# A second queue for the weight loads of the opening: SyncE keeps the transposes, GpSimd issues the loads, with a new order of loads, buffers and sums

## The reference

```python
def _bitlinear(x, w):
    scale = jnp.mean(jnp.abs(w))
    q = jnp.round(jnp.clip(w / (scale + EPS), -1.0, 1.0))
    deq = q * scale
    return x @ deq.T
gate = _bitlinear(hidden_states, w_gate)
up = _bitlinear(hidden_states, w_up)
inter = gate * up
out = _bitlinear(inter, w_down)
x = x + out
```

## Time and profile before

| what | us |
|---|---|
| median of 3 executions (lowest, highest) | 1809.03 (1807.89, 1809.25) |
| the profiled execution's own time | 1808.83 |
| its span | 1807.0 |
| TensorE busy in the span | 1724.9 (95%) |
| VectorE busy | 1096.0 (61%) |
| ScalarE busy | 547.6 (30%) |
| GpSimd busy | 36.1 (2%) |

### The profile page before, as it was taken

The page is one execution under the profiler, slowest core; times in us unless marked ns, Lnnn a source line. Parts: engine busy times, 40 slices in busy tenths (PEclk is TensorE's granted clock), DMA queues, the critical chain, the costliest instruction groups (busy, mean ns, idle before and its releaser), DMA issues.

```text
span 1807.0 us, 29229 instructions
## 1 busy us (share of the span) xinstructions
PE 1724.9 (95%) x11625; PEld 1154.0 (64%) x11625; DVE 1096.0 (61%) x1769; ACT 547.6 (30%) x884; POOL 36.1 (2%) x60
## 2 busy tenths in 40 slices
PE   5775979999999999999999999999999999999999
PEld 3332444444545968678685968769695877768584
DVE  5885984576442645856468555856468455766364
ACT  5536132274210312323132312323032322233030
POOL 0200000010000000000000000000000000000000
PEclk8887989999999999999999999999999999999999
DMA  8679721241102312142123412241022412222021
GB/s 312 209 175 277 188 85 55 95 185 77 67 24 75 115 41 103 62 171 81 38 78 118 147 42 93 72 172 62 21 103 103 151 62 93 72 100 81 21 103 47
DMA packets 92015, 188.62 MB, mean 104 GB/s; under 512 B 41568, under 2 KB 41888, under 8 KB 91872
## 3 DMA queue, kind: packets, MB, share of 16 engines
q1 hardware_dynamic: 89168, 172.13, 28.7%
q0 software_dynamic: 2480, 14.22, 2.0%
q10 hardware_dynamic: 224, 0.28, 0.0%
HBM read 147.07 MB, written 31.01 MB: 99 GB/s over the span
## 4 chain that ended last, share of the span: by engine, by line
PE 86%; DVE 5%; issue 4%; DMA 3%; ACT 1%; SPq 1%; DVEq 0%; ACTq 0%
PE ps L830 43%; PE ps L659 21%; PE ps L887 20%; DVE msk L1307 3%; PE ps L848 2%; DMA inter<-in_L_ffn_w_gate_dram 1%; DVE msk L1311 1%; ACT g_r L1002 1%; DMA wgT<-msk 1%; DVE prod L1339 1%; DMA wuT<-msk 1%; DVE inter L1351 0%; DVE yp L1270 0%; DMA xa<-in_x_dram 0%; SPq L532 0%
## 5 line engine op out<-in xcount | busy, mean ns | idle before, releaser
L830 PE MATMUL ps<-yp,wgT 128*128 128x256 f16 x3528 | 773.6, 273 | 2.6 <-issue 1.4
L830 PE MATMUL ps<-wuT,wgT 128*128 128x256 f16 x3528 | 773.6, 273 | 0.0
L830 PEld LDWEIGHTS ps<-yp,wgT 128*128 128x128 fp8e4 x3528 | 345.3, 98 | 44.4 <-issue 3.4
L830 PEld LDWEIGHTS ps<-wuT,wgT 128*128 128x128 fp8e4 x3528 | 345.3, 98 | 42.8 <-issue 1.6
L887 PE MATMUL ps<-wdT,inter 128*128 128x512 fp8e4 x1680 | 371.3, 379 | 0.0
L887 PEld LDWEIGHTS ps<-wdT,inter 128*128 128x128 f16 x1680 | 163.8, 98 | 194.7 <-issue 1.1
L1605 DVE SCALAR_TENSOR_TENSOR xr<-ps,osc,xr 128x512 f32<-128x512 f32 x180 | 134.1, 748 | 146.5 <-PE ps L887 111.5
L659 PE MATMUL ps<-yp,wgT 128*128 128x512 f16 x672 | 150.8, 388 | 10.1 <-DVE yp L1270 9.8
L659 PE MATMUL ps<-yp,wuT 128*128 128x512 f16 x672 | 150.6, 385 | 4.8 <-DVE prod L1339 4.8
L1554 DVE TENSOR_TENSOR wdT<-ps,msk 128x512 f32<-128x512 f32 (+1 forms) x66 | 44.0, 666 | 177.9 <-PE ps L830 177.9
L659 PE MATMUL ps<-wdT,inter 128*128 128x512 fp8e4 x672 | 147.7, 379 | 0.0
(11 more groups left out here) (197 smaller groups left out, 1530.8 us busy)
## 6 DMA issues: line engine op xcount, KB each, us to landing
wgT<-wcomb SPq DMA_DIRECT2D x60, 896.0 KB, 4.7
wdT<-dcomb SPq DMA_DIRECT2D x12, 2240.0 KB, 9.8
xa<-in_x_dram SPq DMA_DIRECT2D x8, 2048.0 KB, 8.9
out_dram<-xr SPq DMA_DIRECT2D x64, 256.0 KB, 2.0
wdT<-in_L_ffn_w_up_dram SPq DMA_DIRECT2D x10, 512.0 KB, 5.1
wcomb<-raw POOLq DMA_DIRECT2D x11, 448.0 KB, 2.8
ys<-in_L_ffn_w_down_dram SPq DMA_DIRECT2D x9, 512.0 KB, 4.7
wcomb<-msk POOLq DMA_DIRECT2D x10, 448.0 KB, 2.7
```

The source lines that it names most:

```text
L830: last = nc.tensor.matmul(out, w, operand(i, OPERAND[what])[:, k, :], start=(start and h + k + i == 0), stop=(k == KQ - 1 and i == 1), ski ...
```

## The change

- SyncE's queue issues the first 23 loads (the 22 gate tiles and, new, u19 for its sum, into `prod`) and from then on only the 68 transposes, each behind `s_q` of its own tile, and `load_x(1)` and the bias ahead of d20's transpose. Three transposes into `wuT` (u9, u13, u17) also wait for the sum of the last down tile that used the slot there.
- GpSimd's queue issues the other 63 loads, in one list, after its multiplications and the block diagonals. Each waits until its slot's tile before is quantised or summed. They have semaphores of their own (`s_load`).
- The order of the loads and their slots are new: the first sums of down use `wuT` slots 2 to 4, u10 to u18 go to `wd` and `ys`, and a `tail` slot is laid over `ab` and `l1`.
- Sums of up stand at the start and G0 to G9, M(1) behind G11 with the quantising of g21 between it and the total. Sums of down stand at G12 to U2, M(2) at U3 with the quantising of u21 between it and the total of down, which now stands behind U3.
- VectorE quantises tile n at ("T", n), with the entries four places earlier, so that it is as far ahead as before; all sums from there on are on ScalarE as before.
- The `residual` copies move from U15 to U18 to U13 to U16.

The number of loads, sums, transposes, quantised tiles and matmuls is the same.

**First place: SyncE's queue from g7's transpose on, before.** T is a transpose, the L532 rows are weight loads; `wdT`, `ys`, `prod`, `inter` and `raw` name the slots, and the count is at the end.

The core of the diff:

```diff
+    xr, raw0, pr, tail = base[0:4], base[4], ("prod", 0), ("tail", 0)
+    loads = [(n, True, True, s) for n, s in enumerate(wd + base + it + wu)]
+    load(NG, [(19, pr)], quant=False)
+    load(NG, [(10, wd[0]), (4, pr)])
+    load(NG, [(20, yy[0]), (21, yy[1])], quant=False)
+    load(NG, [(17, yy[2]), (18, yy[3]), (11, wd[1]), (12, wd[2]), (15, yy[0]), (16, yy[1]), (13, wd[3]), (14, wd[4]),
+              *zip(range(5, 10), base), *zip(range(4), it[3:])])
+    load(2 * NG, [(9, wu[2]), (10, wu[3]), (11, wu[4]), (12, wu[2]), (13, wu[3]), (14, base[0]), (15, wu[4]),
+                  *zip(range(16, 20), base[1:]), (20, wu[3]), (21, wu[4])], quant=False)
+    load(2 * NG, [(0, xr[0]), (1, xr[1])])
+    load(NG, [(19, wd[0]), (20, wd[1]), (21, wd[2])], summed=False)
+    load(2 * NG, [(2, xr[2]), (3, xr[3]), (4, raw0)])
+    load(2 * NG, [(22, wd[3]), (23, wd[4])], quant=False)
+    load(2 * NG, zip(range(5, 9), yy))
+    load(2 * NG, zip(range(9, ND), [*base, *yy, raw0, *yy, tail]), summed=False)
+    EARLY = NG + 1
...
+    SUMS_AT_GATE = (2, 2, 2, 2, 2, 2, 2, 2, 2, 3, 0, 0, 2, 1, 2, 2, 2, 2, 1, 2, 2)
+    ns = extend("S", ns, 1)
     for f in range(FT):
         order0.append(("G", f))
...
+        ns = extend("S", ns, SUMS_AT_GATE[f])
+        if f == 11:
             order0.append(("M", 1))
+        nt = extend("T", nt, 2 if f < 8 or f > 11 else 1 if f in (8, 11) else 0)
+        if f == 11:
             order0.append(("W", 1))
     for u in range(UP):
         order0.append(("U", u))
-        ns = extend("S", ns, min(4, NQ - ns))
-        if u == 2:
+        ns = extend("S", ns, min((2, 3, 3, 0)[min(u, 3)], NQ - ns))
+        if u == 3:
             order0.append(("M", 2))
+        nt = extend("T", nt, min(1 if u < 4 else 1 + u % 2, (2 * NG if u < 4 else NQ) - nt))
         if u == 3:
             order0.append(("W", 2))
+            nt = extend("T", nt, 1)
...
+            for n in range(NQ):
+                if n == late:
+                    sp.wait_ge(s_xr, NT)
+                    sp.wait_ge(s_y, KH)
+                    load_x(1)
+                    sp.wait_ge(s_ysc, SCD)
+                    sp.wait_ge(s_yscp, KH - SCD)
+                    load_bias(1)
+                transpose(n)
...
+            last_in = {loads[e][3]: e for e in range(EARLY)}
+            for e in range(EARLY, len(loads)):
+                n, s = loads[e][0], loads[e][3]
+                if s in last_in:
+                    n0, _, quant, _ = loads[last_in[s]]
+                    if quant:
+                        pool.wait_ge(s_q, n0 + 1)
+                    else:
+                        act, count = sum_count(summed.index(last_in[s]))
+                        pool.wait_ge(s_sum_act if act else s_sum_dve, count)
+                elif s[0] == "ys":
+                    pool.wait_ge(s_yhi, KH)
+                    pool.wait_ge(s_ylo, KH)
+                last_in[s] = e
+                nc.gpsimd.dma_start(raw(e), tiles[n][0]).then_inc(s_load[s], 16)
...
-                    if n - 15 in range(NT):
-                        residual(0, n - 15)
+                    if n - 13 in range(NT):
+                        residual(0, n - 13)
```

More of the change, by code:

```diff
@@ L59, in adaln_ternary_ffn, with load @@
     base, wd, wu, it, yy = SLOTS
[L60 to L70, removed]
+    xr, raw0, pr, tail = base[0:4], base[4], ("prod", 0), ("tail", 0)
+    loads = [(n, True, True, s) for n, s in enumerate(wd + base + it + wu)]
+    def load(first, more, summed=True, quant=True):
+        loads.extend((first + n, summed, quant, s) for n, s in more)
+    load(NG, [(19, pr)], quant=False)
[11 more added lines that the diff above has]
+    load(2 * NG, zip(range(9, ND), [*base, *yy, raw0, *yy, tail]), summed=False)
     def hidden(n):
         return n if n < NG else (n - 1) % NG
+    EARLY = NG + 1
+    assert len({s for _, _, _, s in loads[:EARLY]}) == EARLY
     summed = [e for e, (n, s, _, _) in enumerate(loads) if s]
@@ L209, in slot @@
                 return raw5[:, :]
+            if which == "tail":
+                return scr[:, :].bitcast(f32)
             if which == "prod":
@@ L503, in transpose @@
                 sp.wait_ge(s_q, n + 1)
+                if NG < n < 2 * NG and hidden(n) in range(0, 20, 4):
+                    e = max(e for e, x in enumerate(loads) if x[3] == ("wu", hidden(n) // 4))
+                    if not loads[e][2]:
+                        sp.wait_ge(s_sum_act, sum_count(summed.index(e))[1])
                 width = -(-cols // (2 * P)) * 2 * P
@@ L506, in transpose @@
                              transpose=True).then_inc(s_te[n % NM], 16)
-            turned = 0
-            last_in = {}
-            for e, (n, _, _, s) in enumerate(loads):
+            for e in range(EARLY):
                 if e in small:
@@ L515, in _ @@
                     load_x(0)
[L516 to L544 removed]
+                sp.dma_start(raw(e), tiles[loads[e][0]][0]).then_inc(s_raw[loads[e][3]], 16)
+            late = min(n for what, n in order0[order0.index(("U", 13 + NT)):] if what == "T")
+            for n in range(NQ):
[7 more added lines that the diff above has]
+                transpose(n)
             store(0)
@@ L615, in raw_arrived @@
             s = loads[e][3]
-            eng.wait_ge(s_raw[s], 16 * sum(x[3] == s for x in loads[:e + 1]))
+            if e < EARLY:
+                eng.wait_ge(s_raw[s], 16)
+            else:
+                eng.wait_ge(s_load[s], 16 * sum(x[3] == s for x in loads[EARLY:e + 1]))
         @block.gpsimd
@@ L1061, in _ @@
                     up(0, n)
-                    if n - 15 in range(NT):
-                        residual(0, n - 15)
-                elif what == "S" and on_act[n]:
+                    if n - 13 in range(NT):
+                        residual(0, n - 13)
+                elif what == "S":
                     raw_sum(n)
@@ L1382, in _ @@
             for what, n in order0:
-                if what == "T" and n + NM not in range(ends[min(n // NG, 2)], ends[min(n // NG, 2)] + NM):
-                    quantise(n + NM)
-                if what == "S" and not on_act[n]:
-                    raw_sum(n)
+                if what == "T":
+                    quantise(n)
                 if what == "M":
```

65 lines of the change are left out of this document (8 added, 57 removed).

## The result

The changed kernel is slightly slower: a median of 1815.97 us (ten runs, 1808.51 to 1822.24) against 1809.24 for the kernel before, run beside it (1807.89 to 1810.44). The ratio is 1.0037, with a 95% interval of 1.0021 to 1.0053. That is 6.7 us or 0.37% more. The forecast was 1786, with a range of its own from 1781 to 1790 and far ends at 1774 and 1799, and "slower" had 0.08.

A forecast was written before the change was run, and what follows sets the result against it. It took TensorE's idle time from 56 to 250 us, behind VectorE's waits for transposes and sums, as the bound. `down(0, 0)` 24.8 us earlier, less 2 for GpSimd's issues, gave 22.8: from 1808.8 to 1786, range 1781 to 1790.

The forecast's parts named there:

- the split called the last: End of VectorE's down-tile work before x: at 254.99 in the kernel before, forecast at 236.7; actually the last split but one.
- Part 1: Gate tiles and total of up: the 10.22 us wait for a transpose goes; first up tile at 104.4, 9.1 us earlier.
- Part 2: Up tiles and sums of down: loads decide M(2), at 160; first down tile at 162.5, 18.3 us earlier.
- Part 3: Down tiles: 24 tiles and 18 products remain, taking 74.2 us from first down tile to last split.
- Part 4: Load of x: issued at about 222, there before VectorE can add; `down(0, 0)` at 244.8, 24.8 us earlier.
- Part 5: GpSimd's load issues beside VectorE's work: a cost of 2 us taken, 0 to 4 in the range.
- Rival C: GpSimd's issue is held while VectorE works; gain gone at 2.55 us per load, 1845 us at 3.3; chance 0.08.
- Rival B: Transposes starve beside the other queue's loads: 8 us in the up phase, 3 at the gate, time 1797; chance 0.18.

The follow-up runs named there:

- the measuring kernel: Only DMAs, nothing of the model: eight transposes of 128 x 1024 fp8, in most settings beside 20 loads of 512 KB; alone a transpose lands in 2.4 us.
- the two mixtures: In the measuring kernel, 20 loads and eight transposes on two queues (34.1 us) and mixed one by one on SyncE's own queue (34.2 us).
- the queue alone: Kernel before, old order and old place of x, only the loads behind the first 22 moved to GpSimd's queue: 1842.44 us, ratio 1.0169.
- the kernel with late x: Changed kernel's order with all loads on SyncE's queue, but x and bias loaded behind the last transposes, as before the change: 1804.09 us.
- each trial with early x: Kernel before with the residual of chunk 0 two up groups earlier and x loaded earlier, at two places among the last transposes: 1807.24 and 1806.95 us.
- The four others on two queues: Changed kernel with each GpSimd load cut in two (1813.75 us), at most two (1822.56) or three (1806.73) loads under way, or six `msk` buffers (1803.89).

## Why the prediction was wrong, step by step

| step | forecast | measured |
|---|---|---|
| first up tile | 104.4 | 122.55 |
| first down tile | 162.5 | 193.09 |
| from there to the end of the split called the last, us | 74.2 | 73.9 |
| from there to `down(0, 0)`, us | 8.1 | 9.2 |
| `down(0, 0)` | 244.8 | 276.15 |

**Part 1 failed** at "Transposes no longer stand behind loads, so the 10.22 us go." That wait did go, but 18.4 us in seven pieces took its place, because the transposes now ran beside the loads. g20, expected at 99.7, was quantised from 118.06 on. ScalarE's sums, named as what would be late next, had nothing to do with it: VectorE had no wait for them at M(1). (The forecast counted a step too many: the row at 60.08 is g1, so g20 is 19 steps later, at 97.7. TensorE bounds the total at 103.3, so this changed nothing.)

**Part 2 failed with it.** The stretch from the first up to the first down tile was to take 58.1 us and took 70.5, with 19.6 us of waits for `wuT`. The step that failed is "The loads come later than that, and they decide." VectorE was to be at M(2) at 151.1, and the loads at 160. In fact VectorE itself came to M(2) only at 189.6 and then waited 0.96 us for ScalarE: it was 18.2 us late at the first up tile, and the 19.6 us of waits used up the 9 us that the forecast left it and 11 more. So the price of the loads, 307 GB/s from a stretch where loads and transposes stood in one queue, did not decide. From 112 to 180 the changed kernel moved 224 GB/s at a share of 0.99. Two queues do not force that, for the measuring kernel moved 20 loads beside eight transposes as fast on two as on one; why the share is so high here is open.

**Part 3** was right within 0.4 us. **Part 4** was right in kind: the load of x was issued 13 us ahead of the split called the last (14.5 were forecast) and took 8.5 us to land; TensorE waited 5.24 us for it, where no wait was forecast, and the stretch behind the last split shrank from 14.6 to 9.2 us where 8.1 were forecast. **Part 5** was too careful: compares at 0.76 us beside issues of 0.53 show no cost. Rival C did not happen. The rule of the Trainium skill that was named with it (SBUF — State Buffer, Who interferes with whom), by which GpSimd cannot write the descriptors of a DMA while VectorE is in a two-port mode, is not borne out by these 0.53 us (no row shows in which mode the compares ran). The 3.1 us are that page's example of a DMA beside a copy on VectorE; no issue here came near them.

**Rival B was the mechanism, and was mis-sized by a factor of more than two.** It was to cost 11 us, and the time stands 30 us above the forecast: 18.2 at the gate and 12.4 in the up phase. Three terms were wrong. A transpose beside a backlog was to take 6.3 us, in which its own 2.4 us were left out; it takes 10 under a full backlog. Of 13 us for the up phase I kept 8, "because the loads wait for VectorE in turn"; 19.6 us were lost there. And nine loads were to cost 3 us at the gate; two bursts cost 15.1, and 3.3 more were lost behind them. The signs for a full backlog were in the order of the change: 22 loads behind one slot. The first burst, eight loads that wait for almost nothing, I did not price at all.

One judgement on a page helped to lose it. The Trainium skill (DMA: Bandwidth & Descriptors, Queues, rings and completion order) says that a DMA engine serves the queues in turn, by packets of some 9 to 17 descriptors. I read this as three turns for a transpose, hence as harmless. But the other queue gets a packet at each turn too. With 13 rows of 4 KB, the middle of its figure, at the 0.16 us a row of the forecast, a turn is 2.1 us, and three turns with the 2.4 us of a transpose alone are 8.7 us, an estimate from that page. By single packets it is 35 x 0.18 + 2.4, also 8.7. The measured 10 us lie above both and do not decide between them; but under either rule B would have stood. What the same page says under "Issuing engines are not separate DMA queues" (a second issuer saves only issue time) agrees with the 34.1 and 34.2 us of the two mixtures.

The chance of slower, 0.08, hung on C alone. B, worked out with its bursts, should have held the other side: by the forecast's own sum, a loss of more than 22.8 us makes the kernel slower.

## What to carry to other kernels

Before small, urgent transfers are given a queue of their own, ask how many large ones will stand in the other: beside a backlog they share the engines, and here took 10 us instead of 2.4, at no gain in throughput. In one queue an urgent transfer stood behind what was issued ahead of it, which the program sets; in two it paid also for loads that the program issued after it. Holding the second queue short helped the transposes and made the loads late. Where an urgent transfer must come late anyway, look first at the buffers ahead of it: two more `msk` buffers gave 6.7 us on one queue.

## What the runs showed that was not expected

Kernels with loads and transposes on two queues vary more from run to run: 1808.51 to 1822.24 for the changed kernel, 1834.96 to 1844.43 for the queue alone, against 1794.86 to 1795.78 and 1788.59 to 1789.09 on one queue with the new order. These are ten and five executions against five and four; the nine of the kernel with late x, on one queue, span 2.6 us (1802.50 to 1805.13) and the eleven of each trial with early x 3.3 and 2.9, so part of the difference may be the number of executions. The four others on two queues span 4.3 to 8.4 us. Why they vary is open.

The DMA engines are also busier for fewer bytes. From 56 to 250, the changed kernel, then the new order on one queue:

```profile
56.00:250.00 194.00, 150.08 (x660) 66.27 (x661) 150.18 (x202) 74.48 (x136) 36.54 (x65) 0.89 0.85 195
```

```profile
56.00:250.00 194.00, 162.16 (x712) 73.91 (x713) 166.07 (x232) 77.81 (x140) 0.00 (x0) 0.90 0.78 215
```

A share of 0.85 for 195 GB/s against 0.78 for 215: a high DMA share does not show that the engines are well used. What keeps the engines busy without bytes no run shows. And cutting each load into two DMAs gave 17% more packets on their queue, not twice as many.
